# Second attention of a two-layer Flamingo block: attention weights transposed by DMA instead of by TensorE, with a third buffer of logits, and slot zeroing moved into the setup

## The reference

```python
q = _fq_sym(q, axis=-1)
k = _fq_sym(k, axis=-1)
v = _fq_sym(v, axis=2)
attn = jnp.einsum('bhqd,bhkd->bhqk', q, k)
attn = jax.nn.softmax(attn.astype(jnp.float32), axis=-1)
attn = _fq_unsigned(attn, axis=-1)
out = jnp.einsum('bhqk,bhkd->bhqd', attn, v)
out = jnp.transpose(out, (0, 2, 1, 3)).reshape(B, N, C)
return out @ Wp + bp
```

## Time and profile before

| | us |
|---|---|
| median of 3 runs | 1030.58 |
| lowest and highest | 1027.38, 1032.69 |
| the profiled execution | 1020.56 |
| its span | 1018.8 |
| PE, DVE, ACT, POOL busy in it | 826.1, 741.0, 475.5, 653.6 |

### The profile page before, as it was taken

One profiled execution on the slowest core, in us unless ns is written; L12 is line 12 of the kernel. 1 busy time (PEld: TensorE's weight loads), 2 busy tenths in 40 slices (PEclk: granted clock), 3 DMA queues, 4 the chain that ended last, 5 costly groups with the idle time before them and its releaser, 6 DMA issues.

```text
span 1018.8 us, 20963 instructions
## 1 busy us (share of the span) xinstructions
PE 826.1 (81%) x6776; PEld 560.1 (55%) x6777; DVE 741.0 (73%) x1654; ACT 475.5 (47%) x1078; POOL 653.6 (64%) x834
## 2 busy tenths in 40 slices
PE   4489758789998969888878887876869999999952
PEld 2267544566655536555555554544557777775621
DVE  5778768666757688878987889875858777773424
ACT  3355344233322366777676677753414344342310
POOL 3486973566366777887787787851035444468886
PEclk8689969899999955776686876785979999999977
DMA  7031124245433141221310100002014444455556
GB/s 264 19 87 51 50 86 139 61 149 154 125 101 94 56 144 57 93 70 42 113 28 18 44 13 17 6 2 84 6 45 132 133 140 127 143 153 109 72 79 134
DMA packets 72542, 87.64 MB, mean 86 GB/s; under 512 B 11268, under 2 KB 65288, under 8 KB 72456
## 3 DMA queue, kind: packets, MB, share of 16 engines
q1 hardware_dynamic: 57480, 57.40, 17.5%
q0 software_dynamic: 14976, 29.14, 12.7%
HBM read 64.03 MB, written 32.98 MB: 95 GB/s over the span
## 4 chain that ended last, share of the span: by engine, by line
PE 26%; POOL 16%; DVE 13%; issue 8%; POOLq 4%; DVEq 3%; ACT 2%; DMA 1%; ACTq 0%
PE PS L261 11%; DVE sb_slotv L1389 4%; POOL sb_stg L709 4%; PE PS L804 4%; POOL sb_wqp L709 2%; POOL sb_xnf L709 2%; PE PS L1270 2%; DVE sb_wkh L1394 2%; PE PS L767 2%; PE PS L1260 2%; PE PS L796 1%; PE PS L743 1%; PE PS L398 1%; DVE sb_x_sb L899 1%; DMA sb_xnf<-slot_table,sb_place 1%
## 5 line engine op out<-in xcount | busy, mean ns | idle before, releaser
L664 POOL DMA_INDIRECT sb_xnf<-token_table,sb_ids x120 | 115.9, 966 | 161.9 <-DVE sb_ids L578 74.3
L1389 DVE TENSOR_REDUCE sb_slotv<-PS 128x1 f32<-128x512 f32 x256 | 163.7, 681 | 26.6 <-PE PS L1260 26.6
L261 PE MATMUL PS<-sb_xnT,sb_sgu 128*128 128x512 f16 x528 | 125.0, 389 | 1.1 <-DVE sb_lg L446 0.6
L261 PE MATMUL PS<-sb_region,sb_wkh 128*128 x720 | 121.7, 321 | 4.6 <-issue 2.2
L1344 ACT ACTIVATE sb_wk<-PS,sb_slotv 128x512 f32<-128x512 f32 x128 | 87.0, 690 | 24.5 <-DVE sb_slotv L1389 24.2
L261 PEld LDWEIGHTS PS<-sb_region,sb_wkh 128*128 128x128 f16 x720 | 69.4, 100 | 46.0 <-issue 12.9
L827 ACT ACTIVATE sb_wk<-PS 128x512 f32<-128x512 f32 (+1 forms) x48 | 28.6, 596 | 132.8 <-PE PS L261 120.5
L1728 POOL TENSOR_SCALAR sb_wk<-sb_wk 128x512 f32<-128x512 f32 x128 | 79.3, 620 | 16.6 <-ACT sb_wk L1344 7.1
L743 PE MATMUL PS<-sb_sdn,sb_wkh 128*128 128x256 f16 x544 | 68.5, 276 | 24.9 <-DVE sb_wkh L918 22.5
L261 PEld LDWEIGHTS PS<-sb_xnT,sb_sgu 128*128 128x128 f16 x528 | 52.0, 100 | 58.3 <-issue 6.5
L1394 DVE TENSOR_SCALAR sb_wkh<-PS 128x1024 f16<-128x1024 f16 x112 | 76.6, 684 | 8.5 <-PE PS L1282 8.4
(11 more groups left out here) (295 smaller groups left out, 1995.3 us busy)
## 6 DMA issues: line engine op xcount, KB each, us to landing
slot_table<-sb_wa SPq DMA_DIRECT2D x60, 256.0 KB, 2.3
slot_table<-token_table SPq DMA_DIRECT2D x16, 640.0 KB
sb_stg<-gu SPq DMA_DIRECT2D x24, 352.0 KB, 3.5
sb_stg<-dn SPq DMA_DIRECT2D x24, 256.0 KB, 2.9
token_table<-sb_xnf SPq DMA_DIRECT2D x16, 256.0 KB, 3.7
sb_stg<-sgu SPq DMA_DIRECT2D x8, 352.0 KB, 5.1
sb_x_sb<-x SPq DMA_DIRECT2D x1, 2048.0 KB, 12.3
out<-sb_x_sb SPq DMA_DIRECT2D x16, 128.0 KB
```

What stands on the lines that cost most here:

```text
L261: last = nc.tensor.matmul(out_, lhs(i, c), rhs(j, c), start=(c == 0 and n == 0 and not begun), stop=(c == C - 1 and n == 2 and not more))
L664: nc.gpsimd.indirect_dma_start(xg[l][:, 2 * (g % XR) + n, :], None, xw[l][:, :], bass.IndirectOffsetOnAxis(ap=ids[:, 2 * g + n:2 * g + n + ...
L1389: nc.vector.tensor_reduce(h_nb[u][:, h:h + 1], PS[:, 2 * u + h, :], AX, ALU.max, negate=True).then_inc(h_max, 1)
```

## The change

In the second attention the rounded weights no longer go through PE and PSUM. ACT's bias now holds ln 255 besides the maximum, so the exponential is already 255 times as large; POOL adds and subtracts the rounding constant and writes a compact f16 tile `h_p`, a ring of four; SP issues one DMA transpose a step from `h_p` to `h_T`, also a ring of four; PE's weighted sums read `h_T` five steps behind. `values` and both `copies` are gone. The two PSUM banks that they used are a third pair for the logits, and PE issues logits two steps ahead. ACT's buffers `h_e` go from four to three. DVE writes the two maxima of a step to a small tile, drains, and adds ln 255 in a second instruction; ACT waits for it. The rings lie partly in `xnf`, which the last combinations of layer 0 still read, so POOL and SP wait for those at s = 2. The weight items of the attention are issued by SP between the transposes. The 16 transfers of `zero_slots` go to the setup: four behind each pair of experts' loads.

```diff
-FRAC = 1.0 / (255.0 * 128.0)
+LEVELS = math.log(255.0)
+FRAC = 1.0 / 128.0
...
-        STEPS = NQ + PAIRS + 1
-        RB, RB_BITS = 1024.0, float(0x6400)
-        ON_ACT = (1,)
-
-        def act_copies(n):
-
-            return n // PAIRS * len(ON_ACT) + sum(1 for p in ON_ACT if p < n % PAIRS)
-
-        def wait_copied(eng, n):
-
-            if act_copies(n) > 0:
-                eng.wait_ge(h_pc_act, act_copies(n))
-            if n - act_copies(n) > 0:
-                eng.wait_ge(h_pc_dve, n - act_copies(n))
+        STEPS = NQ + PAIRS + 3
+        AHEAD, BEHIND = 2, 5
+
+        def wait_transposed(eng, n):
+
+            if n >= 0:
+                eng.wait_ge(h_pT[n % 4], 16 * (n // 4 + 1))
...
-        h_nb = [small[:, 10 + u, 0:2] for u in range(2)]
+        h_nb = [small[:, 10 + u, 0:2] for u in range(3)]
+        h_top = [small[:, 13 + u, 0:2] for u in range(2)]
...
-        h_e = [wk1[:, 0:2], wk1[:, 2:4], xnf[:, 8:12, :].rearrange("p t d -> p (t d)").rearrange("p (h k) -> p h k", h=2),
-               wkh[:, 0:4].rearrange("p a b -> p (a b)").bitcast(F32).rearrange("p (h k) -> p h k", h=2)]
+        h_e = [wk1[:, 0:2], wk1[:, 2:4], xnf[:, 8:12, :].rearrange("p t d -> p (t d)").rearrange("p (h k) -> p h k", h=2)]
         NE = len(h_e)
 
-        h_p = [e.bitcast(F16)[:, :, ::2] for e in h_e]
-        h_T = [wkh[:, 4 + 2 * u:6 + 2 * u].rearrange("p a b -> p (a b)") for u in range(2)]
+        h_h = [wkh[:, 2 * u:2 * u + 2].rearrange("p a b -> p (a b)") for u in range(4)] + \
+            [xnf[:, 2 * u:2 * u + 2, :].rearrange("p t d -> p (t d)").bitcast(F16) for u in range(4)]
+        h_p, h_T = h_h[0::2], h_h[1::2]
...
             def logits(s):
-                t, pair, u = s // PAIRS, s % PAIRS, s % 2
+                t, pair, u = s // PAIRS, s % PAIRS, s % 3
                 if pair == 0:
                     at_least(pe, q_ready, 0, t + 1)
                 for h in range(2):
-                    at_least(pe, h_exp, 0, 2 * (s - 2) + h + 1)
+                    at_least(pe, h_exp, 0, 2 * (s - 3) + h + 1)
                     r = slice(64 * h, 64 * h + 64)
                     nc.tensor.matmul(PS[:, 2 * u + h, :], q_iT[t % 3][r, pair, :], kT[pair // 4][r, pair % 4, :],
                                      start=True, stop=True).then_inc(h_qk, 1)
 
-            def values(s):
-                u = s % 2
-                wait_copied(pe, s - 1)
-                bank = PS[:, 4 + u, :].bitcast(F16)
-                for h in range(2):
-                    at_least(pe, h_int, 0, 2 * s + h + 1)
-                    for k in range(KT):
-                        last = nc.tensor.transpose(bank[:, (h * KT + k) * P:(h * KT + k + 1) * P],
-                                                   h_p[s % NE][:, h, k * P:(k + 1) * P], idh[:, :])
-                last.then_inc(h_pT, 1)
-
             def weighted(s):
-                u, pair = s % 2, s % PAIRS
-                wait_copied(pe, s + 1)
+                t, pair = s // PAIRS, s % PAIRS
+                wait_transposed(pe, s)
                 if pair == 0:
-                    at_least(pe, o_norm, 0, s // PAIRS)
+                    at_least(pe, o_norm, 0, t)
                 for h in range(2):
                     head = 2 * pair + h
                     for k in range(KT):
-                        last = nc.tensor.matmul(PS[:, 6, D + head * HD:D + (head + 1) * HD],
-                                                h_T[u][:, (h * KT + k) * P:(h * KT + k + 1) * P],
+                        last = nc.tensor.matmul(PS[:, 6, head * HD:(head + 1) * HD],
+                                                h_T[s % 4][:, (h * KT + k) * P:(h * KT + k + 1) * P],
                                                 Vi[:, k, head * HD:(head + 1) * HD], start=(k == 0), stop=(k == KT - 1))
                 last.then_inc(h_pv, 1)
...
-            logits(0)
+            for s in range(AHEAD):
+                logits(s)
+            at_least(pe, s_accr[0], 0, BLK)
             for s in range(STEPS):
-                t, pair = s // PAIRS, s % PAIRS
-                if s + 1 < NQ:
-                    logits(s + 1)
-                if s == 1:
-                    at_least(pe, s_accr[0], 0, BLK)
-                if 2 <= s < NQ + 2:
-                    values(s - 2)
-                if 4 <= s < NQ + 4:
-                    weighted(s - 4)
+                if s + AHEAD < NQ:
+                    logits(s + AHEAD)
+                if BEHIND <= s < NQ + BEHIND:
+                    weighted(s - BEHIND)
...
             def exponentials(s):
-                u, pair, v = s % 2, s % PAIRS, (s // PAIRS) % 2
-                at_least(act, h_pT, 0, s + 1 - NE)
+                u, pair, v = s % 3, s % PAIRS, (s // PAIRS) % 2
+                at_least(act, h_max, 0, s + 1)
                 for h in range(2):
                     head = 2 * pair + h
-                    at_least(act, h_max, 0, 2 * s + h + 1)
+                    at_least(act, h_int, 0, 2 * (s - NE) + h + 1)
                     nc.scalar.activation(h_e[s % NE][:, h, :], PS[:, 2 * u + h, :], ACT.Exp, bias=h_nb[u][:, h:h + 1],
                                          accum_out=o_sum[v][:, head:head + 1]).then_inc(h_exp, 1)
-
-            def copies(s):
-                at_least(act, h_pT, 0, s + 1)
-                at_least(act, h_pv, 0, s - 1)
-                nc.scalar.activation(h_T[s % 2], PS[:, 4 + s % 2, :].bitcast(F16), ACT.Copy, bias=-RB).then_inc(h_pc_act, 1)
...
             def maxima(s):
-                u = s % 2
+                u = s % 3
                 for h in range(2):
                     at_least(dve, h_qk, 0, 2 * s + h + 1)
-                    at_least(dve, h_exp, 0, 2 * (s - 2) + h + 1)
-                    nc.vector.tensor_reduce(h_nb[u][:, h:h + 1], PS[:, 2 * u + h, :], AX, ALU.max, negate=True).then_inc(h_max, 1)
-
-            def copies(s):
-                at_least(dve, h_pT, 0, s + 1)
-                at_least(dve, h_pv, 0, s - 1)
-                nc.vector.tensor_scalar(h_T[s % 2], PS[:, 4 + s % 2, :].bitcast(F16), -RB, None, ALU.add).then_inc(h_pc_dve, 1)
...
-                if 3 <= s < NQ + 3 and (s - 3) % PAIRS not in ON_ACT:
-                    copies(s - 3)
-                if pair == 4 and 1 <= t <= NT:
+                if pair == BEHIND and 1 <= t <= NT:
...
+        def attn1_sp(sp):
+            for s in range(NQ):
+                at_least(sp, h_int, 0, 2 * s + 2)
+                at_least(sp, h_pv, 0, s - 3)
+                if s == 2:
+                    at_least(sp, c_used[0], 0, NT)
+                sp.dma_start_transpose(h_T[s % 4].rearrange("p (g n) -> p g n", n=P), h_p[s % 4]).then_inc(h_pT[s % 4], 16)
+                n, part = split_turn(s - 1)
+                if part == 1 and n + 4 < len(items):
+                    load_item(sp, n + 4)
...
-            steps(sp, E[0] // 2, 1, 0, 0, two_experts)
+            sp.wait_ge(zeroed[1], 16)
+            for s in range(E[0] // 2):
+                two_experts(0, s)
+                for n in range(4):
+                    zero_slots(sp, 4 * s + n)
             for n in range(4):
                 load_item(sp, n)
             table_dma(sp, 0)
             for n in range(4, FIRST_ITEMS + 4):
                 load_item(sp, n)
             rows_dma(sp, 0)
-            sp.wait_ge(zeroed[1], 16)
-            for n in range(LATER_ITEMS + 4, len(items)):
+            for n in range(LATER_ITEMS + 4, BEFORE_KEYS + 4):
                 load_item(sp, n)
-                if n < LATER_ITEMS + 4 + ZERO_PARTS:
-                    zero_slots(sp, n - LATER_ITEMS - 4)
+            attn1_sp(sp)
...
             def integers(s):
+                wait_transposed(pl, s - 4)
+                if s == 2:
+                    at_least(pl, c_used[0], 0, NT)
                 for h in range(2):
                     at_least(pl, h_exp, 0, 2 * s + h + 1)
-                    nc.gpsimd.tensor_scalar(h_e[s % NE][:, h], h_e[s % NE][:, h], 255.0, MAGIC + RB_BITS,
-                                            ALU.mult, ALU.add).then_inc(h_int, 1)
+                    nc.gpsimd.tensor_scalar(h_p[s % 4][:, h * CTX:(h + 1) * CTX], h_e[s % NE][:, h], MAGIC, -MAGIC,
+                                            ALU.add, ALU.add).then_inc(h_int, 1)
```

27 lines of the change are left out of this document (15 added, 12 removed).

## The result

| | before | changed |
|---|---|---|
| median of the 4 runs each, us | 1028.98 | 1315.41 |
| lowest, highest | 1025.53, 1032.69 | 1313.85, 1316.34 |
| the profiled execution, its span | 1020.56, 1018.8 | 1313.85, 1311.6 |

The ratio is 1.278, with a 95% interval of 1.273 to 1.283: 286 us slower. The forecast of 1023.5 was wrong in sign, and the time lies far outside the range of 1006 to 1105.

The account below looks back on a forecast made before the run. POOL was taken as nearest to the bound in the second attention. Attention -15.5, tail +1.5 and setup +7 gave -7 us, taken from the median of 1030.58 to 1023.5 us; range 1006 to 1105.

Parts of the forecast that it names:

- The step that failed: POOL's rounding in the second attention: writing f16 into another tile was to cost nothing extra.
- The bound: Second attention: POOL is nearest to the bound, with 292.0 us without its waits for ACT, 2.28 us a step.
- The gain of 15.5 us: Second attention: POOL loses most of its 26.0 us of waits for ACT, making the attention 15.5 us shorter.
- ACT now starts a pair only when both maxima are there: Second attention: ACT starts about 0.9 us later, hidden by three buffers of logits.
- under 10: Sign of being right: POOL's waits for ACT between first and last rounding come to under 10 us.
- a long stretch on PE or DVE: Second attention: with two logits buffers such stretches (queries, output) pass on at once; POOL waits 2.78 us after one.
- the 7 us that I forecast: Whole kernel: the sum of the terms, 7 us faster than before.
- The setup, 7 us: Setup: zeroing behind the expert loads delays layer 0's routed experts by 7 us, bounds 0 and 14.
- The transposes, 1 to 2 us each and hidden: Second attention: 128 DMA transposes of 256 KB, 1 to 2 us each, hidden if under about 2.3 us.
- Rival 1: Second attention: DMA transposes take over 2.3 us each and set the pace, 1054 to 1233 us; chance 0.33.
- The tail, +1.5 us: End of the second attention: the last pair's way through the DMA adds 1.5 us, bounds 0 and 4.
- POOL's second wait, +3: Second attention: POOL's added wait each step for the transpose four steps back costs 3 us, bounds 0 and 9.

Follow-up runs that it names:

- e2: Changed kernel with POOL's rounding replaced by (mult 1, add 0), so rounding to integers is left out: 1030.80 us, kernel before 1029.65.
- e4: Changed kernel with rounding by (mult 1, add 1024) into f16, PE taking the offset off, zeroing with partitions outermost: 1029.53 us, before 1029.65.
- e12: e4 again, word for word, to time it: 1020.41 us against 1022.53 for the kernel before, ratio 0.998.
- e10: e4 with DVE's query_fractions one step later, behind the next maxima, and POOL's integer steps at 8 and 9: 1010.77 us, ratio 0.988 to before.
- e8: e4 with two pairs of logits banks in place of three, logits issued one step ahead: 1035.56 us, ratio 1.0125 to before.
- e3: Kernel before with only the 16 zeroing transfers moved to the setup, in their old form: 1036.61 us against 1030.46, ratio 1.0059.
- e1: Kernel before with POOL's rounding as (add, add) in place of (mult, add), factor 255 left out: 1311.95 us against 1029.65.
- e11: Kernel before with only query_fractions one step later and POOL's integer steps at 8 and 9: 1025.46 us, ratio 1.002 to before.
- e9: e4 with POOL's parts of the queries one step earlier, except the first tile's integers: 1034.81 us against 1030.46 for before, ratio 1.0035.
- e6: e4 with every logits matmul issued twice into the same bank: 1030.22 us against 1030.46 for the kernel before, ratio 1.000.

## Why the prediction was wrong

**The step that failed** is "POOL. The rounding writes f16 into another tile in place of f32 in the same one. The two forms cost the same in the splits: 0.78 us for 704 columns either way. So nothing." It looked at the output and the tile, which indeed cost nothing (e2: 621 ns), and not at the operations. The two rows that I compared are both (mult, mult); the old rounding is (mult, add); the new is (add, add), a pair that POOL nowhere runs in the kernel before. It was an operation that the trace doesn't show, and had to be bounded from both sides and put among the rivals. No rival of mine had it either. The term was +333 us of POOL's work (256 x 1.30), and 281 us in the length of the attention. The diff had the hint: a multiplication by a constant gave way to a second addition on the one engine with the least slack. The kernel before also writes its round trip through the constant on POOL as two instructions with a multiplication by 1.0 in the second (`query_integers`), and on DVE as one (add, add).

**The bound was right.** POOL sets the end of the attention: without its waits for ACT it needs 290.5 us in e4, 290.7 in e12 and 291.9 in e10, where I had read 292.0. So of its 325 us of added busy time, all came out in the length but the 44 us of idle time that it swallowed.

**The gain of 15.5 us** needs two statements. As the value of the third pair of banks it measured 15.6 us (e8 against e12); that the two numbers agree is luck, since mine was meant against the kernel before. As that difference it was 3.5 to 5 us (314.5 and 313.1 against 318.0), since the rest of the new chain costs about 12 us. The prediction had seen that ACT now starts a pair only when both maxima are there, and took it as hidden by the third buffer. That is one candidate; the third buffer of exponentials in place of four, and PE at a lower clock, are others. They weren't tried one by one, so this cause is open. The waits left (23.8 us in e12, where I had said under 10) come for the most part from DVE's list, which the prediction named as the origin ("a long stretch on PE or DVE") without asking whether more logits could help past it.

**What would be left without the pair** is not the 7 us that I forecast. e12 is at 0.998 of before with the zeroing in its better form; with the zeroing of the change, which costs 6.1 us in e3, I estimate some 4 us more than before.

**The setup, 7 us**: 6.1 by e3 (3.6 to 8.7), gathers 8.9 us later in the changed kernel. The pieces: POOL's stop of 12.74 us (13.5 predicted), deviations 2.2 us late at 136.89 (137.1), the one-hot step at 180.85 (181.5). The path was followed correctly. The spread over 5 engines, which the Trainium skill (DMA: Bandwidth & Descriptors, "Why a DMA increments its semaphore by 16 and not by 1") gives from the shapes, is borne out by the share of 0.33 in the earlier trace rows, about 5 of 16, and by e4, where partitions outermost cut the first quartet from 14.5 us to 3.3.

**The transposes, 1 to 2 us each and hidden**: 1.47 us, issue 1.23 us, landing 3.1 us. Right; "issued in under 1 us" was a little low. Rival 1 had 0.33 of the chance and deserved less: at 1.47 us it never decides.

**The tail, +1.5 us**: from POOL's last rounding to the deviations it is 983.00 - 969.89 = 13.1 us. In the kernel before it was 692.01 - 677.91 = 14.1, so nothing was added:

```profile
692.01 2.91 POOL L1802 TENSOR_TENSOR sb_rstd<-sb_ve,sb_mhalf 128x16 f32<-128x16 f32 x1 [14.09 <-DVE sb_ve L251]
```

**POOL's second wait, +3**: it cost nothing that can be seen. No wait of POOL for a transpose appears in e4's list, where POOL has its old pace, and two roundings there take 1.32 us, against 1.31 before.

**The start.** The profiled execution of before began its attention at 359.90; e1 and e11, with the same setup, began at 365.84 and 365.08. The changed kernel began at 371.05; e2 and e3, with the same zeroing, at 377.10 and 376.27. So one setup scatters by 5 to 6 us from execution to execution, but the distance of 11 us is there in either pairing. Why it is more than the 6.1 us that e3 loses in the whole stays open; e3's attention itself is no more than 1.3 us shorter than that of before (316.7 against 318.0).

## What to carry to other kernels

Price an instruction on GpSimd by its pair of operations, not by its shape and types alone: a row is a comparison only if it runs the same pair, and a pair that the trace doesn't show is an unknown with two bounds. A constant round trip x + M - M was three times as dear here as (mult 1, add c) into a type whose spacing does the rounding. And before a buffer is added to take up stalls, read one stall from its end to its start: if an in-order engine stands with ready work behind a wait, the buffer helps in full only together with the order (e10 against e12). The longest total in a list of waits may cost nothing (e9). And an experiment that makes an instruction cheap must keep its pace too: compare two in a row, not one (e2 against e4).

## What the runs showed of the hardware

- On GpSimd, a `tensor_scalar` of 128x512 takes 0.62 to 0.68 us for (mult, add) and 1.92 to 1.94 for (add, add), for f32 and f16 alike (one sample of 2.75 apart). In one sample each, f32 only, (add, mult) took 0.62, (mult, subtract) 1.96 and one add alone 1.50. Why, no run shows.
- Two such roundings in a row took 1.31 to 1.32 us with (mult, add of a constant that is not 0), and 1.20 to 1.22 with (mult 1, add 0), at 0.62 us each in both. Why, no run shows.
- A DMA transpose of 128x1024 f16 inside SBUF: issue 1.23 us, landing 3.1 us, one each 1.47 us when they stand in a row and the DMA engines are full, with no measurable slowing of POOL's instructions beside it (621 ns).
- TensorE with a doubled stream of logits was granted 0.65 to 0.69 in place of 0.54 to 0.61 (e6 and e4, stretches of 400 to 660 us), means between the levels of 1.2 and 2.4 GHz, and the time was the same.
- Four transfers of 640 KB with an outermost size of 5 are issued in 14.2 to 18.1 us, and the load behind them in 5.31 (the change, e3). With the 128 partitions outermost it is 2.8 to 4.0 us, and 1.3 to 1.7 for a load that follows at once (e4, e12).
